# Expert choice one sequence at a time, with the spreading ten pieces behind its own pair

## What is computed

```python
k = Sx // num_experts * CAPACITY            # 746 // 16 * 2 = 92
logits = jnp.einsum('bsd,de->bse', x, gate_weight)
affinity = jax.nn.softmax(logits, axis=-1).transpose(0, 2, 1)
gating, index = jax.lax.top_k(affinity, k)
x_in = jnp.take_along_axis(x[:, None, :, :], index[..., None], axis=2)
h = jax.nn.gelu(jnp.einsum('bekd,edh->bekh', x_in, w1) + b1[None, :, None, :])
x_e = jnp.einsum('bekh,ehd->bekd', h, w2) + b2[None, :, None, :]
weighted = gating[..., None] * x_e
out = out.at[jnp.arange(Bx)[:, None], idx_flat].add(vals_flat)
```

## Time and profile before

| | before |
|---|---|
| median of 3 runs | 2249.67 us (2248.93 to 2251.78) |
| profiled execution | 2256.49 us |
| its span, first to last instruction | 2254.7 us |
| PE busy in the span | 2007.5 us (89%) |
| DVE, ACT, POOL busy | 1592.4, 1071.6, 617.4 us |
| mean granted TensorE clock | 0.96 |

### The profile page before, as it was taken

The page is one execution under the profiler, slowest core; times in us unless marked ns, Lnnn a source line. Parts: engine busy times, 40 slices in busy tenths (PEclk is TensorE's granted clock), DMA queues, the critical chain, the costliest instruction groups (busy, mean ns, idle before and its releaser), DMA issues. The chain is left out here.

```text
span 2254.7 us, 54559 instructions
## 1 busy us (share of the span) xinstructions
PE 2007.5 (89%) x20890; PEld 1780.6 (79%) x20890; DVE 1592.4 (71%) x4080; ACT 1071.6 (48%) x2699; POOL 617.4 (27%) x664
## 2 busy tenths in 40 slices
PE   8699999999637888886999999987999999999998
PEld 6497777778536878885777777766999999999998
DVE  5746566554683855674999999977777777777774
ACT  4433333332434555553677766753444444444443
POOL 0202222210025545510333333333222212221220
PEclk9799999999878999997999999998999999999999
DMA  8100110000211111100000000000000000000000
GB/s 186 44 1 13 13 13 11 11 6 1 81 55 39 44 32 40 41 15 1 3 3 3 3 3 3 3 2 1 8 14 7 7 11 10 7 7 14 7 8 15
DMA packets 80547, 44.50 MB, mean 20 GB/s; under 512 B 45865, under 2 KB 74089, under 8 KB 80009
## 3 DMA queue, kind: packets, MB, share of 16 engines
q1 hardware_dynamic: 73416, 29.26, 5.7%
q0 software_dynamic: 5888, 12.07, 2.0%
q10 hardware_dynamic: 1024, 0.26, 0.1%
HBM read 27.20 MB, written 14.38 MB: 18 GB/s over the span
## 5 line engine op out<-in xcount | busy, mean ns | idle before, releaser
L2130 ACT ACTIVATE w<-banks,b 128x384 f32<-128x384 f32 (+1 forms) x512 | 259.6, 572 | 392.7 <-PE banks L2205 392.7
L2187 PE MATMUL banks<-w,w 128*128 128x128 f32 (+1 forms) x3072 | 364.1, 275 | 0.0
L2187 PEld LDWEIGHTS banks<-w,w 128*128 128x128 f32 (+1 forms) x3072 | 350.4, 189 | 9.1 <-issue 8.7
L1713 PE MATMUL banks<-qT,w 64*64 64x128 f32 (+1 forms) x4608 | 268.1, 269 | 13.1 <-DVE eb L1615 8.7
L1713 PEld LDWEIGHTS banks<-qT,w 64*64 64x64 f32 x4608 | 247.5, 134 | 30.9 <-issue 20.8
L1721 PE MATMUL banks<-eb,w 64*64 64x128 f32 (+1 forms) x4608 | 268.9, 270 | 1.0 <-DVE eb L1615 1.0
L1684 POOL TENSOR_TENSOR t<-eb 128x768 f32<-128x768 f32 x96 | 171.7, 1789 | 289.6 <-ACT eb L1661 287.0
L1721 PEld LDWEIGHTS banks<-eb,w 64*64 64x64 f32 x4608 | 244.1, 133 | 1.7 <-DVE eb L1615 1.5
L2027 DVE SCALAR_TENSOR_TENSOR h<-banks,t_wt,h 128x128 f32 (+3 forms) x672 | 183.6, 341 | 82.5 <-PE banks L2187 79.0
L1240 POOL DMA_INDIRECT xg<-xs,rowu x184 | 179.8, 977 | 127.2 <-DMA xg<-xs,rowu 85.0
L1615 DVE TENSOR_TENSOR eb<-eb,rd 128x1536 f32<-128x1536 f32 x96 | 210.8, 2196 | 2.3 <-ACT rd L1672 2.3
(11 more groups left out here) (305 smaller groups left out, 4246.2 us busy)
## 6 DMA issues: line engine op xcount, KB each, us to landing
out<-h SPq DMA_DIRECT2D x16, 320.0 KB
xs<-r_xl SPq DMA_DIRECT2D x16, 192.0 KB, 2.9
xg<-xs,rowu POOLq DMA_INDIRECT x184
h<-in_xT SPq DMA_DIRECT2D x3, 750.0 KB, 14.4
h<-in_xT SPq DMA_DIRECT2D x3, 749.0 KB, 17.4
xs<-r_xl SPq DMA_DIRECT2D x16, 128.0 KB
blocks<-NT SPq DMA_DIRECT2D x24, 48.0 KB, 1.9
D<-blocks SPq DMA_DIRECT2D x24, 48.0 KB, 2.0
```

What stands on the lines that cost most here:

```text
L1713: last = nc.tensor.matmul(lbanks(n)[place(n, hd), v, 0:wide(n)], k.Kt[half(hd), v, :], qT[half(hd), n // NC % 2, (n % NC) * P:(n % NC) * P ...
L2130: nc.scalar.activation(gb[u % 2][:, f, s * GW:s * GW + NFREE[s]], k.ps[:, order.bank(n), 0:NFREE[s]], ACT.Relu, bias=k.b1_1[:, 2 * e + f:2 ...
L2187: last = nc.tensor.matmul(k.psf[0:n, o:o + P], gb[u % 2][:, f, c * P:c * P + n], k.w2_1[:, 2 * e + f, :], start=(f == 0), stop=(f == 1))
```

## The change

One expert's unit now covers 92 rows of one sequence. There are 32 `hidden` and 32 `output` units a pair, each 92 columns wide, and experts 0 to 15 of the first sequence come before those of the second (`x % E0` picks the weights). A batch is four neighbouring tiles, so ACT copies it with one instruction and not two. The list is laid out by pieces: each of its 202 slots holds one piece of spreading and then a twenty-fourth of a front, two or three units. The front of pair q starts after piece 14 of pair q-1 and ends after piece 13 of pair q. The first ten slots have no spreading and the last ten no front. `turned` comes three pieces ahead of its first piece, where it was four. `rows` 1 moves from piece 18 to piece 8 of pair 2. The waits and banks stay as they were. The core of the diff:

```diff
@@ class ExpertOrder @@
     BATCHES = 6
+    EXPERTS = 2 * E0
+    LEAD = 14
...
+        self.batch = [range(4 * g, min(4 * g + 4, self.TILES)) for g in range(self.BATCHES)]
...
-        for e in range(E0 + 2):
-            if e < E0:
+        for e in range(self.EXPERTS + 2):
+            if e < self.EXPERTS:
...
-        for u in self.front():
-            out.append((0,) + u)
-            if u == ("output", max(self.experts_for(t) for t in range(4)) - 1):
-                out.append((0, "turned", 0))
-        pieces = self.pieces()
-        for p in range(PAIRS):
-            front, done = self.front() if p + 1 < PAIRS else [], 0
-            for n, (tile, par, lo, hi) in enumerate(pieces):
-                if lo == 0 and tile % 4 == 0:
-                    if tile // 4 + 1 < self.BATCHES:
-                        out.append((p, "turned", tile // 4 + 1))
-                    elif p + 1 < PAIRS:
-                        out.append((p + 1, "turned", 0))
+        pieces, front = self.pieces(), self.front()
+        N = len(pieces)
+        first = {n: tile // 4 for n, (tile, par, lo, hi) in enumerate(pieces) if lo == 0 and tile % 4 == 0}
+        for at in range(self.LEAD - N, PAIRS * N):
+            p, n = divmod(at + 3, N)
+            if n in first and 0 <= p < PAIRS:
+                out.append((p, "turned", first[n]))
+            if at >= 0:
+                p, n = divmod(at, N)
+                tile, par, lo, hi = pieces[n]
                 out.append((p, "spread", n))
...
-                if (p, n) == (2, 18):
+                if (p, n) == (2, 8):
                     out.append((p, "rows", 1))
-                upto = len(front) * (n + 1) // len(pieces)
-                out += [(p + 1,) + u for u in front[done:upto]]
-                done = upto
+            q, m = divmod(at + N - self.LEAD, N)
+            if q < PAIRS:
+                for u in front[len(front) * m // N:len(front) * (m + 1) // N]:
+                    out.append((q,) + u)
...
@@ ACT, gathered @@
-                        nc.scalar.activation(xgT[:, lows[0]:lows[-1] + 1, :],
-                                             k.ps[:, 0, 0:len(lows) * P].rearrange("p (t s) -> p t s", s=P), ACT.Copy)
...
+                        nc.scalar.activation(xgT[:, 4 * x:4 * x + order.count(x), :],
+                                             k.ps[:, 0, 0:order.count(x) * P].rearrange("p (t s) -> p t s", s=P),
+                                             ACT.Copy).then_inc(t_moved, 1)
...
@@ PE, hidden @@
-                        nc.tensor.matmul(k.ps[:, 3, 0:EW].rearrange("p (b n) -> p b n", b=2),
-                                         k.w1_0[:, x, :], flat[:, :, x * CAP:(x + 1) * CAP],
+                        nc.tensor.matmul(k.ps[:, 3, 0:CAP], k.w1_0[:, x % E0, :], flat[:, x * CAP:(x + 1) * CAP],
                                          start=True, stop=True).then_inc(hid_ps, 1)
```

More of the change, by code:

```diff
@@ L931 @@
     BATCHES = 6
+    EXPERTS = 2 * E0
+    LEAD = 14
     def __init__(self):
[L934 to L939, removed]
+        self.batch = [range(4 * g, min(4 * g + 4, self.TILES)) for g in range(self.BATCHES)]
     def count(self, g):
-        return len(self.batch[g][0]) + len(self.batch[g][1])
+        return len(self.batch[g])
     def batch_of(self, tile):
-        return next(g for g, (lo, hi) in enumerate(self.batch) if tile in lo or tile in hi)
+        return tile // 4
     def batches_for(self, e):
[L949 to L954, removed]
+        return self.batch_of((e * CAP + CAP - 1) // P) + 1
     def experts_for(self, tile):
[L958 to L961, removed]
+        return (tile * P + P - 1) // CAP + 1
     def parts(self, tile):
@@ L1061, in expert_choice_phase @@
         xgT = sb("xgT", [P, TILES, P])
-        hid = sb("hid", [P, 4, EW])
+        hid = sb("hid", [P, 4, CAP])
         yh = sb("x_yh", [P, 8, C], F32R)
@@ L1077, in expert_choice_phase @@
         xs_b = k.xs.rearrange("(b t) d -> b t d", t=T)
[L1078 to L1081 removed]
+        flat = xgT[:].rearrange("p t s -> p (t s)")
+        EX = order.EXPERTS
         def turned_tiles(p, g):
@@ L1236, in _ @@
                             pool.wait_ge(t_ps, (p - 1) * order.BATCHES + g + 1)
-                        lows, highs = order.batch[g]
-                        for j, tile in enumerate(lows + highs):
+                        for j, tile in enumerate(order.batch[g]):
                             col = column(p, tile)
@@ L1302, in _ @@
                         act.wait_ge(t_ps, p * order.BATCHES + x + 1)
-                        lows, highs = order.batch[x]
-                        nc.scalar.activation(xgT[:, lows[0]:lows[-1] + 1, :],
-                                             k.ps[:, 0, 0:len(lows) * P].rearrange("p (t s) -> p t s", s=P), ACT.Copy)
-                        nc.scalar.activation(xgT[:, highs[0]:highs[-1] + 1, :],
-                                             k.ps[:, 0, len(lows) * P:order.count(x) * P].rearrange(
-                                                 "p (t s) -> p t s", s=P), ACT.Copy).then_inc(t_moved, 1)
+                        nc.scalar.activation(xgT[:, 4 * x:4 * x + order.count(x), :],
+                                             k.ps[:, 0, 0:order.count(x) * P].rearrange("p (t s) -> p t s", s=P),
+                                             ACT.Copy).then_inc(t_moved, 1)
                     elif kind == "hidden":
-                        n = p * E0 + x
+                        n = p * EX + x
                         act.wait_ge(hid_ps, n + 1)
@@ L1313, in _ @@
                             act.wait_ge(o_ps, n - 3)
-                        nc.scalar.activation(hid[:, n % 4, :], k.ps[:, 3, 0:EW],
-                                             ACT.Gelu_apprx_tanh, bias=k.b1_0[:, x:x + 1]).then_inc(hid_ready, 1)
+                        nc.scalar.activation(hid[:, n % 4, :], k.ps[:, 3, 0:CAP], ACT.Gelu_apprx_tanh,
+                                             bias=k.b1_0[:, x % E0:x % E0 + 1]).then_inc(hid_ready, 1)
                     elif kind == "output":
-                        n = p * E0 + x
+                        n = p * EX + x
                         act.wait_ge(o_ps, n + 1)
@@ L1322, in _ @@
                             act.wait_ge(y_ps, (p - 1) * order.BATCHES)
-                        nc.scalar.activation(expert_major(p)[:, :, x * CAP:(x + 1) * CAP],
-                                             k.ps[:, 4, 0:EW].rearrange(
-                                                 "p (b n) -> p b n", b=2),
-                                             ACT.Identity, bias=k.b2_0[:, x:x + 1]).then_inc(o_ready, 1)
+                        nc.scalar.activation(yT[p % 2][:, x * CAP:(x + 1) * CAP], k.ps[:, 4, 0:CAP], ACT.Identity,
+                                             bias=k.b2_0[:, x % E0:x % E0 + 1]).then_inc(o_ready, 1)
                     elif kind == "turned":
@@ L1406, in _ @@
                             pe.wait_ge(o_ready, n)
-                        nc.tensor.matmul(k.ps[:, 4, 0:EW], k.w2_0[:, x, :],
+                        nc.tensor.matmul(k.ps[:, 4, 0:CAP], k.w2_0[:, x % E0, :],
                                          hid[:, n % 4, :], start=True, stop=True).then_inc(o_ps, 1)
@@ L1410, in _ @@
                         tiles = turned_tiles(p, x)
-                        pe.wait_ge(o_ready, p * E0 + max(order.experts_for(t) for t in tiles))
+                        pe.wait_ge(o_ready, p * EX + max(order.experts_for(t) for t in tiles))
                         n = p * order.BATCHES + x
```

9 lines of the change are left out of this document (4 added, 5 removed).

## The result

The changed kernel took 2364.52 us (median of 5 runs, 2357.59 to 2371.15); the kernel before, beside it, 2249.92 us (5 runs, 2248.93 to 2254.30). The ratio is 1.0499, 95% interval 1.0475 to 1.0523: 115 us slower. The forecast was 2320, range 2286 to 2345. The direction was right, the time lies outside the range, and 45 of the 115 us were not foreseen.

The account below looks back on a forecast made before the run. The prediction took PE as close to full, with POOL's 38.0 us a pair a second floor. It summed 63 + 360.5 + 12 = 435.5 us against 365.5, 70 more, so a median of 2320 us, range 2286 to 2345.

Parts of the forecast that it names:

- front of pair 0: Start of the stage: first piece near 690, fourteen more slots, front ending 63 us after the first transfer.
- a pair, seven of them: Middle of the stage: 51.5 us a pair, 360.5 us for seven instead of 288.1.
- last ten pieces: End of the stage: ten pieces of spreading left without a front, taken as 12 us.
- PE's narrow unit: On PE: 0.24 us for 92 columns because weights still load, 5.5 us more a pair.
- Rival 1: On PE: weight load hidden, unit 0.155 us, round trip stays; 47.8 us a pair, +42, 2292; chance 0.10.
- the round trip: PE to ACT and back: 0.96 us between units of a kind, 0.48 idle each, in 16 of 24 slots.
- Rival 2: PE does not stand at the trip through ACT: 41 us a pair, 2241, or 2222 with half price; chance 0.07.
- what gets no dearer: ACT under 30 of 51.5 us, DVE unchanged, POOL's 38.0 below 51.5 so its waits vanish, 48.22 us pair shrinks.
- Rival 4: turned three pieces ahead makes DVE's selections late: 3 us a pair, +91, 2341; chance 0.07.
- rival 3: PE idle a quarter of the time lowers the clock to 0.90: 27 us more, 2347; chance 0.06.
- the likeliest case: The summed forecast itself, with 48.5 to 54 us a pair: 2298 to 2337 us; chance 0.70.

Follow-up runs that it names:

- three14: Changed kernel with hidden and output taking turns on three PSUM banks, turned on bank 1 alone: 2239.27 us, ratio 0.9952 to the kernel before.
- turned1: Changed kernel with turned on PSUM bank 1 alone and nothing else: 2355.93 us, ratio 1.0484 to the kernel before.
- lead0: Changed kernel with LEAD 0 instead of 14, spreading a whole pair behind the front: 2360.52 us, ratio 1.0483 to the kernel before.
- warm14: Changed kernel, turned on bank 1 alone, unread identity transposes where PE would wait for a unit's bank: 2323.69 us, ratio 1.0325 to the kernel before.
- split14b: Changed kernel, first unit behind a piece moved between its halves, except where a piece ends a sequence: 2356.39 us, ratio 1.0430 to the kernel before.
- before_rows8: Kernel before with only rows 1 moved from piece 18 to piece 8 of pair 2, and its two waits: 2241.83 us, ratio 0.9958.
- three0: Changed kernel with narrow units on three banks in turn, turned on bank 1, and LEAD 0: 2264.39 us, ratio 1.0064 to the kernel before.
- wide3: Kernel before with rows 1 early and its wide units on three banks in turn: 2240.73 us, ratio 0.9966 to the kernel before.

## Why the prediction was right in direction and short in size

Its terms, with what the traces give for them (pair 0's front begins at 658.79, its first transfer, 2.5 us later than in the kernel before; the ends are pieces 14 of pairs 0 and 7 on PE's timeline):

```profile
726.32 0.66 PE L1408 MATMUL banks<-x_sel,x_yh 128*128 128x374 f32 x1
...
1113.97 0.66 PE L1408 MATMUL banks<-x_sel,x_yh 128*128 128x374 f32 x1
```

| term | forecast | measured | how |
|---|---|---|---|
| front of pair 0 | 63 | 67.5 | 726.32 - 658.79 |
| a pair, seven of them | 51.5 | 55.4 | (1113.97 - 726.32) / 7 |
| last ten pieces | 12 | 11.75 | 1125.72 - 1113.97 |
| stage | 435.5 | 466.9 | 1125.72 - 658.79 |

The stage is 101.4 us longer than before's 365.5, 31.4 more than my 70. Of these 27.2 lie in the pairs, 4.5 in the front. The medians differ by 114.6, since the profiled execution of before was a high one of its kernel and that of the changed kernel the lowest of its five. So of the 45 us that were not foreseen 31 are the stage's; the other 14 lie in which executions were profiled, and no step of the prediction accounts for them.

*Right: PE's narrow unit.* Half the columns don't take half the time, because the weights are loaded as before. I took 0.24 us by the earlier trace rows; it is 0.19 to 0.23 where units follow each other, 4.2 us of PE's time a pair and not 5.5. Rival 1, a hidden load, would have 0.155 and falls.

*Right: the round trip is the large term.* Slot 1.91 against 1.89, PE's wait on ACT in 144 places, some twenty a pair. `three14` takes away the waits for the one bank of each kind (and one of the two banks of `turned`, which by `turned1` costs nothing) and with them the whole loss. Rival 2 falls. The trip was 0.87 and not 0.96, the unit cheaper, the piece dearer; the full-clock pairs of `lead0`, 51.4, and of `warm14`, 50.85, against 51.5 say that the small errors nearly cancel. That is in part luck. So is one comparison: for the wide units it held the trip of 1.15 against 1.0 of work, by which the trip would not be covered; from start to start the work is 0.31 + 0.31 + 0.69 = 1.31, and it is. And the cost of the trips in sum is less well understood than their price in one slot: by the same reckoning `split14b` should have taken most of it away, and did not.

*Right: what gets no dearer.* No wait on fetched tiles, none of the long pair at the place where the second list came late, ACT 30.1 busy of 54.7, the end 11.75. The first piece came at 693.08, forecast near 690, and 2.5 of that is the later start. Rival 4 is not seen: one wait on a selection in all, 0.4 us.

*The step that failed* is rival 3, "The clock falls", with a chance of 0.06 and outside the sum. The prediction set it aside because "the steps of 697.04 to 701.64 had PE busy 3.45 of 4.60 us, also a quarter idle, and the clock stayed 1.00". That stretch is 4.6 us long, and I let it stand for 360. In the changed kernel the grant stays at 1.00 for tens of us at a time, then falls in every pair for some 12 us, and a pair takes 54.7 us where at full clock it takes 51.4 (`lead0`). The price that the rival gave, 27 us for a clock of 0.90, is near the 27.2 of the pairs, whose grant is 0.91 in four of the six, 0.94 and 0.83 in the others. `warm14` against `turned1` gives 32 to 36 for the pairs, the front and the end together (the end's last 20 us stand at 0.76, and in the front too PE's grant is low). It was never a rival to the round trip, for in the full pairs of the changed kernel and its variants it came with the waits: with them gone, in `three14`, every pair runs at 1.00, and with them filled, in `warm14`, all but one of the six do. Nor do the waits always bring it, as `lead0` shows. But a price of 27 us that hangs on the likeliest case belongs in its sum or wholly in the range.

*Mis-sized with it:* the front. Its 14 slots after the first piece were priced at 29.5 us, some 2 of it for the slow clock, and took 33.2 (693.08 to 726.32); the row of 690 to 719 has 0.84.

*The parts of the change, one by one:* the earlier list is worth -9.5 us (`before_rows8`). Narrow units cost PE 4.2 us a pair, 30 in all, by busy time, and 22 in time (`three0` against `wide3`). The lag gives 25 back where it can (`three0` against `three14`); in the changed kernel it gives next to nothing, since shorter ends are paid for by the clock in the pairs (`lead0`). The sum of these three is -12.5, near the -10.8 of `three14`. The round trip with the clock costs 125 (`three14` against the changed kernel, by the medians; 5.5% by the ratios), of it 32 to 36 the clock.

The version that beats both kernels is `three14`, 0.5% under the kernel before. `before_rows8` comes within 0.1% of it, and their intervals overlap: one moved line, with its two waits, is worth nearly as much as the whole change set right.

## What to carry to other kernels

A unit that goes through PE, another engine and back in one bank has a floor of one round trip (0.87 us here for 92 columns, 1.06 for 184), so before units are halved or reordered, ask for each one how much of other work PE has before the next of its kind; where it is less, give a third bank. Moving work in between is not sure to do the same (`split14b`). When a sum leaves PE idle in short, regular gaps, put the lower clock into the range at least, and don't take a stretch of a few microseconds as proof that it stays up. Measure the small separable edits of a change alone: here one line held most of the gain.

## What the runs showed of the hardware

In the changed kernel the granted clock fell in every pair. In the one shown no wait was over 0.7 us before the fall: PE was busy 19.84 of 23.10 us (863.70 to 886.80) at 1.00, then came 0.56 for 11.59 us. It stayed at 1.00 in five of six full pairs with the gaps filled by transposes (`warm14`), but also through 141.77 us of `lead0` with PE busy 118.53 and 55 of the same waits. So short gaps can bring the clock down and need not, and no rule can be read from these runs. The Trainium skill, TensorE: Matmul & The Clock Gate, section A second HAM failure mode: psum-queue depth-cycling, describes a kernel whose short idles between matmul groups swing the clock between its two levels; the changed kernel's trace agrees, that of `lead0` only in some of its pairs. I had read the clock from one row and not weighed that section.

A record of 92 columns with a full load of weights stands 0.095 to 0.115 us from the next where units follow each other in `three14`, less than the 0.121 and 0.123 of the earlier trace rows, though those stream fewer columns. What the groups of the earlier trace rows waited for besides was not looked into.
